# Message products in partition quarters, the copy of the sums moved between distances and one-hots, and GpSimd without its wait for landed gathers

## The reference

```
h = relu(layernorm(x))
for each of 3 layers:
    W[e]   = (edge_attr[e] @ ew + eb) as a 16x16 matrix      # one matrix for each edge
    msg[e] = h[src[e]] @ W[e]
    h      = segment_sum(msg, dst) + h @ rw + rb
    layers 1 and 2: batch norm over the nodes; all: relu
out = x + h @ pred_w + pred_b
```

## Time and profile before

| | |
|---|---|
| median of 3 runs | 7843.1 us (7841.94 to 7845.44) |
| the profiled execution's own time | 7844.59 us |
| its span, first to last instruction | 7842.8 us |
| mean granted TensorE clock | 0.978 |
| PE / PEld busy | 94% / 84% |
| DVE / POOL / ACT busy | 75% / 68% / 64% |

### The profile page before, as it was taken

One profiled execution on the slowest core, in us unless ns is written; L12 is line 12 of the kernel. 1 busy time (PEld: TensorE's weight loads), 2 busy tenths in 40 slices (PEclk: granted clock), 3 DMA queues, 4 the chain that ended last, 5 costly groups with the idle time before them and its releaser, 6 DMA issues.

```text
span 7842.8 us, 135584 instructions
## 1 busy us (share of the span) xinstructions
PE 7377.1 (94%) x51692; PEld 6562.7 (84%) x51692; DVE 5875.9 (75%) x7566; ACT 5020.2 (64%) x8367; POOL 5324.6 (68%) x5635
## 2 busy tenths in 40 slices
PE   4999999999999899999999999999999999999998
PEld 2888888888888688888888888868888888888887
DVE  3777777777777677777777777767777777777775
ACT  3666666666666466666666666656666666666665
POOL 4677777777777377777777777737777777777772
PEclk7999999999999799999999999989999999999998
DMA  7111111111111111111111111111111111111110
GB/s 37 29 30 30 30 30 30 30 30 30 30 28 29 26 30 30 28 30 30 30 30 30 30 30 30 29 25 29 30 30 30 30 27 30 30 30 30 30 30 20
DMA packets 783265, 229.16 MB, mean 29 GB/s; under 512 B 643869, under 2 KB 733869, under 8 KB 782619
## 3 DMA queue, kind: packets, MB, share of 16 engines
q1 hardware_dynamic: 529252, 172.27, 10.7%
q0 software_dynamic: 180000, 46.44, 6.9%
q10 hardware_dynamic: 73367, 1.76, 1.0%
HBM read 216.52 MB, written 3.52 MB: 28 GB/s over the span
## 4 chain that ended last, share of the span: by engine, by line
PE 66%; ACT 28%; issue 2%; DVE 2%; DMA 1%; DVEq 1%; ACTq 0%
PE bank L1074 57%; ACT distance L914 13%; ACT low_hot L918 13%; PE bank L1088 2%; PE bank L1030 2%; PE bank L1089 2%; ACT z L878 1%; PE bank L1097 1%; PE bank L1098 1%; DMA key_all<-in_src 1%; PE bank L1143 1%; DVE xbig L638 1%; PE bank L1155 1%; DVEq L719 0%; DVE agg L724 0%
## 5 line engine op out<-in xcount | busy, mean ns | idle before, releaser
L468 POOL DMA_INDIRECT xg<-node_table,idx x5625 | 5323.8, 946 | 2394.5 <-issue 1768.1
L1074 PE MATMUL bank<-nodes,low_hot 128*128 128x400 f32 x30000 | 5729.9, 348 | 25.0 <-DVE nodes L651 15.1
L1074 PEld LDWEIGHTS bank<-nodes,low_hot 128*128 128x128 f32 x30000 | 5401.4, 188 | 285.0 <-issue 254.8
L914 ACT ACTIVATE distance<-key_all,low_id 128x640 bf16<-128x640 int16 x3000 | 2242.6, 818 | 2056.8 <-issue 1298.9
L683 DVE TENSOR_TENSOR spread<-mask,bank 128x400 f32<-128x400 uint8 x3750 | 2015.5, 565 | 1571.9 <-PE bank L1074 1571.6
L918 ACT ACTIVATE low_hot<-distance,one 128x640 fp32r<-128x640 bf16 x3000 | 2231.0, 815 | 0.0
L688 DVE TENSOR_REDUCE xg<-spread 128x80 f32<-128x2000 f32 x750 | 1677.3, 2236 | 25.7
L638 DVE TENSOR_TENSOR xbig<-xg,bank 128x1280 f32<-128x1280 f32 x750 | 1327.4, 1810 | 1.0 <-issue 0.2
L1041 PE MATMUL bank<-xbig,hot 128*32 128x144 f32 x18750 | 992.6, 294 | 0.0
L1041 PEld LDWEIGHTS bank<-xbig,hot 128*32 128x32 f32 x18750 | 819.7, 109 | 163.6 <-issue 101.3
L1088 PEld LDWEIGHTS bank<-merge,z 128*128 128x128 f32 x942 | 146.7, 188 | 428.2 <-ACT z L878 422.8
(11 more groups left out here) (109 smaller groups left out, 1031.3 us busy)
## 6 DMA issues: line engine op xcount, KB each, us to landing
key_all<-edge_keys SPq DMA_DIRECT2D x375, 320.0 KB, 3.7
xg<-node_table,idx POOLq DMA_INDIRECT x5625
ea<-in_edge_attr SPq DMA_DIRECT2D x375, 100.0 KB
idx<-in_src SPq DMA_DIRECT2D x375, 7.5 KB
node_table<-rows_room SPq DMA_DIRECT2D x3, 781.2 KB
xbig<-node_table SPq DMA_DIRECT2D x9, 192.0 KB
xbig<-in_x SPq DMA_DIRECT2D x2, 781.2 KB
xbig<-in_dst ACTq DMA_DIRECT2D x1, 782.5 KB, 68.1
```

Source lines behind the costliest of these rows:

```text
L468: pool.indirect_dma_start(out=xg[u][:, j, :], out_offset=None, in_=table[:, :], in_offset=bass.IndirectOffsetOnAxis(ap=idx[u][:, j:j + 1], ...
L914: nc.scalar.activation(distance[f][:, 0:tiles.stop - tiles.start, :], key[u % KEYS][:, tiles, :], ACT.Abs, bias=low_id[:, f:f + 1]).then_i ...
L1074: last = nc.tensor.matmul(p_sel[t % BANKS], low_hot[:, f, t, :], nodes[i][:, f, :, :].rearrange("p d f -> p (d f)"), start=(f, i) == (0, 1 ...
```

## The change

Three edits.

1. `messages_of` no longer makes two matmuls of 500 columns for a full quad, but two of 100 columns for each of its five rounds. Rounds 0 to 3 write to partitions 0, 32, 64 and 96 on, in the same 100 columns, round 4 to partition 0 on in the next 100 columns: first the four `w_now` products, then the four `eb_now` products, then round 4's two. VectorE's additions read the quarters.
2. ScalarE's `copy_rounds` for group g moves from the head of group g+1 into group g, behind the four distances of the second half of group g+2 and ahead of their four one-hots.
3. The wait for landed gathers ahead of GpSimd's eighth gather is gone.

```diff
-        p_agg = bank[2][0:D, 0:QROUNDS * SPAN].rearrange("d (q w) -> d q w", w=SPAN)
+        p_agg = [bank[2][q % GANG * WIN:q % GANG * WIN + D, q // GANG * SPAN:(q // GANG + 1) * SPAN]
+                 for q in range(QROUNDS)]
...
                         for j in range(FETCHED):
-                            if j == BREATH and b * SLOTS + u:
-                                landed(pool, layer, b * SLOTS + u - 1)
                             pool.indirect_dma_start(
...
-                    nc.vector.tensor_tensor(here, here, p_agg[:, r % QROUNDS, :], ALU.add).then_inc(s_add, 1)
+                    nc.vector.tensor_tensor(here, here, p_agg[r % QROUNDS], ALU.add).then_inc(s_add, 1)
...
-            def compare_keys(layer, b, u, half):
+            def compare_keys(layer, b, u, half, between=None):
...
                     nc.scalar.activation(distance[f][:, 0:tiles.stop - tiles.start, :], key[u % KEYS][:, tiles, :], ACT.Abs,
                                          bias=low_id[:, f:f + 1]).then_inc(s_dist, 1)
+                if between is not None:
+                    copy_rounds(layer, between)
                 for f in range(FOLD):
...
                         g = b * SLOTS + u
-                        if g:
-                            copy_rounds(layer, g - 1)
                         copy_picked_rows(layer, b, u)
                         copy_fetched_rows(layer, b, u)
                         if g:
                             copy_transposed(layer, g - 1)
                         if not (last and u >= SLOTS - 2):
                             compare_keys(layer, b, u + 2, 0)
-                            compare_keys(layer, b, u + 2, 1)
-                copy_rounds(layer, G - 1)
+                            compare_keys(layer, b, u + 2, 1, between=g)
+                        else:
+                            copy_rounds(layer, g)
                 copy_transposed(layer, G - 1)
...
-                to = p_agg[:, 0:count, :].rearrange("d q w -> d (q w)")
-                nc.tensor.matmul(to, w_now[:], zT[:, 0:count, :].rearrange("p q w -> p (q w)"), start=True, stop=False)
-                nc.tensor.matmul(to, eb_now[:], zxT[:, 0:count, :].rearrange("d q w -> d (q w)"),
-                                 start=False, stop=True).then_inc(s_mm, 1)
+                for first in range(0, count, GANG):
+                    some = range(first, min(first + GANG, count))
+                    for q in some:
+                        nc.tensor.matmul(p_agg[q], w_now[:], zT[:, q, :], start=True, stop=False)
+                    for q in some:
+                        last = nc.tensor.matmul(p_agg[q], eb_now[:], zxT[:, q, :], start=False, stop=True)
+                last.then_inc(s_mm, 1)
```

More of the change, by code:

```diff
@@ L33 @@
 TURNS = 3
-BREATH = 7
 TRIPLE = 3
```

## The result

| | before | changed |
|---|---|---|
| median | 7842.5 us (4 runs, 7839.84 to 7845.44) | 7480.4 us (4 runs, 7477.05 to 7482.27) |
| ratio, 95% interval | | 0.9538, [0.9521, 0.9554] |
| span of the profiled execution | 7842.8 us | 7479.3 us |
| mean granted clock | 0.978 | 0.979 |

The change saves 362 us; 340 were forecast (7503 us). Two of the four chips on which experiments ran (0 and 2 in the record, against 8 and 1) held TensorE back: there the kernel before took 11,500 us instead of 7842, so each run is compared with the kernel before on its own chip.

The account below looks back on a forecast made before the run. TensorE, busy 958 of 999 us, was taken as the bound, with small pauses left to win. Moved copy 293 us, quartered messages 47 and GpSimd's wait 0 sum to 340: 7843 - 340 = 7503 us, range 7430 to 7610.

Parts of the forecast that it names:

- Edit 2, 1.05 us in 279 groups, 293 us: Moved copy ends TensorE's pause for `z` before the transposes: 1.05 us in each of 279 groups, 293 us.
- N: Plain group, timed between starts of TensorE's sums: 19.07 us before, forecast 18.02.
- Q: Group with two transposed rounds and messages: 21.83 us before, 20.78 with the moved copy, 20.3 with both edits.
- the price of an unhindered round: Two picks and a transposed round without a pause, 3.59 us in Q's second round, against 4.64 with the pause.
- A: Group after Q, 19.29 us on average; the copy's gain is hidden there behind VectorE's register loads and additions: 0.
- the prediction's own aside: In A, VectorE's additions end at about 6.1 us, so even TensorE's transposes would wait 0.6 us.
- Edit 1, 0.51 us a quad, 47 us: Quartered messages on TensorE in Q: 1.87 us falls to 1.36, 0.51 us in 93 full quads, 47 us.
- Edit 3, nothing: GpSimd's wait before the eighth gather holds nothing up, so removing it gains 0.
- GpSimd is close but not the bound: After the change TensorE needs 75.6 us a quad, GpSimd 74.9; TensorE stays the bound by 0.7 us.
- the rival at 0.09: GpSimd becomes the bound, keeping 0.35 us of waiting at each group's head: 68 us more, 7571 us; chance 0.09.
- the rival that I gave 0.04: Granted clock falls because TensorE pauses less, making the kernel slower: about 7980 us at a mean of 0.92; chance 0.04.
- The rival on VectorE: VectorE bounds plain groups, losing half of 1.05 us in 62 a layer, or additions double: about 7600 us; chance 0.09.

Follow-up runs that it names:

- the early additions: Changed kernel, VectorE's offset loads moved behind its reduction of the picks' first half and its five additions behind pick t = 7: 7366.1 us, ratio 0.9391.
- the last two experiments: The early additions on the changed kernel (7366.1 us), and that kernel with each group's first tile gathered again into a spare buffer, sixteen gathers (7800.4 us, ratio 0.9947).

## Why the prediction was right, point by point

- **Edit 2, 1.05 us in 279 groups, 293 us.** Right in mechanism and size: 296 us alone, N at 18.01 us and Q at 20.77 with the old messages on the mean, 1.06 us less each. Taking the price of an unhindered round from Q, rather than the 0.8 us of bare waiting, was what made the size right; 279 x 0.8 would have been 223 us.
- **A gives nothing.** Right: 19.28 us after, 19.26 before, on the mean of all 90. In the rows shown it takes 1.31 us more than a plain group. TensorE's wait for VectorE's L681 reads only 0.52 us, not the "over 1 us" I named: the transposes already wait for the additions there (0.28 us, in the prediction's own aside 0.6). The remaining half microsecond is in the matmuls around the two waits; the transposes' row is 0.44 us there and 0.36 in a plain group, which would fit weight loads that are no longer hidden. The early additions show the cause: they took 114 us out of these 90 groups, 1.27 us each.
- **Edit 1, 0.51 us a quad, 47 us.** Mechanism right, the term mis-sized: 0.74 us a quad, 64 us alone. I priced eight quartered matmuls at the sums' 0.103 us each, as if a fixed price held for them; in the new trace four cost 0.29 us, 0.07 each, and the whole stretch 1.13 us where I had 1.36. The Trainium skill's span model (TensorE: Matmul & The Clock Gate, section Measured speedup vs the span model: one matmul's duration and 4 ns for each further one) gave about 1.1 us for the whole stretch, and 1.13 were measured. Its other rule, about 60 cycles of overhead for each matmul (TensorEngine Tiling (Array Packing), section Instruction Overhead), can't be seen in quarters; a 0.27 us matmul of 100 columns in series has room for it. This term is most of the miss of 23 us: 0.23 us in 93 quads are 21 us, and the messages alone gained 17 us more than I gave them. That VectorE's additions cost nothing more from the quarters was right too: five take 1.78 us with the early additions, 1.77 in the kernel before.
- **Edit 3, nothing.** Right: unhindered, putting the wait back changed nothing, and on the chips that hold back taking it out changed nothing. The trace of the kernel with the wait put back has no row of GpSimd waiting for landed gathers.
- **GpSimd is close but not the bound.** Right, and on firmer ground than my argument. GpSimd still waits at the heads of groups, 76.0 us in all, where it was 411.9. I compared paces (75.6 against 74.9 us a quad) and called the lead a buffer for single groups. The lead also carries a difference in pace through a whole layer, as the last two experiments show, so the rival at 0.09 would have cost less than I priced it: its 0.18 us a group are 22 us a layer, and the lead is over 30.
- **The granted clock.** 1.00 in the long stretches, as forecast, unhindered. On the other two chips the rival that I gave 0.04 holds with its sign: the kernels in which TensorE is fuller unhindered are the slower ones there, and edits 1 and 2 together are a loss of 6%. I had looked for it in the clock alone, which is lower on the mean (0.818 in the copy alone, 0.835 in the kernel before); most of the lost time is standing still (2893 of 4547 us).
- **A miscount.** The rival on VectorE counts 62 plain groups a layer; there are 63 (189 in all). It moves that rival by 1 us and the forecast not at all.

## What to carry to other kernels

When a wait is taken off a nearly full engine, read the price of the unwaited step from a place where it already happens unwaited, and then look for the group in which another engine's delay sits at the same point: there the gain is nothing until that delay goes too. A producer that is a few per cent too slow can still be free of charge if it starts each phase with a lead; compare its deficit over the phase with the lead, not pace with pace. And time a kernel that fills TensorE on more than one chip: the same two edits gave 0.954 on one and 1.061 on another.

## What the runs showed of the hardware that was not expected

- Four matmuls of 128x16 by 100 columns in different partition quarters took 0.29 us together, one alone 0.27 us.
- A chip can hold TensorE back within one program so that single records of the sums start 0.7 to 2.8 us apart for some 14 us, after picks at a granted clock of 1.00. The kernel before is 47% slower there, at a mean granted clock of 0.83 to 0.84 against 0.98.
- Indirect gathers came every 1.25 us over a whole layer (1875 of them in 2343 us, in the kernel with the early additions, which has no wait for landed ones); with that wait, in the kernel before, fifteen took 18.73 us, the same pace.
